# A graph layer on one core: only row tiles and one weight first, and the last layer norm from a row sum and a sum of squares

## The reference

```python
xn = layernorm(x)                                  # no gain, eps 1e-5
y  = segment_sum(edge_weight[:, None] * xn[src], dst) @ Wg + bg
q, k = elu(xn @ Wq + bq) + 1, elu(xn @ Wk + bk) + 1    # 8 heads of 64
v  = xn @ Wv + bv
mix = (q @ (k.T @ v)) / (q . sum(k)) @ Wp + bp         # per head
x  = x + y + mix
z  = layernorm(x)
g  = mean over rows(relu(z @ gfc1.T + b) @ gfc2.T + b) # 8 gates
W1m = W1 + sum_e g_e tv_W1[e];  W2m = W2 + sum_e g_e tv_W2[e]   # biases too
r  = z + relu(z @ W1m.T + b1m) @ W2m.T + b2m
out = x + (r - mean(r)) * rsqrt(var(r) + eps) * lng + lnb
```

## Time and profile before

| | us |
|---|---|
| device time, median of 3 runs | 1880.41 (1877.25 to 1880.98) |
| profiled execution, device time | 1881.32 |
| its span | 1879.5 |
| busy: TensorE, VectorE, POOL, ScalarE | 1549.2, 1212.1, 919.1, 702.8 |
| opening, head loop, k phase, q phase, last pass (from stretches) | 39, 200, 538, 579, 190 |

### The profile page before, as it was taken

How to read it: one execution, slowest core, us unless ns; L and a number is a source line. 1 busy time by engine, 2 the same in 40 slices (tenths; PEclk the granted TensorE clock), 3 DMA queues, 4 the chain that set the end, 5 groups by cost and what they waited for, 6 DMA issues and landing times.

```text
span 1879.5 us, 27602 instructions
## 1 busy us (share of the span) xinstructions
PE 1549.2 (82%) x8551; PEld 672.3 (36%) x8551; DVE 1212.1 (64%) x2230; ACT 702.8 (37%) x1098; POOL 919.1 (49%) x919
## 2 busy tenths in 40 slices
PE   0699968888988898787888888888887799888883
PEld 0345423333333333243333333333333444453331
DVE  7888734554544555456776777676667666468996
ACT  3266522222222232212332333333333677425554
POOL 3000056666666666646666666666663000016776
PEclk9799989999999999978999999999999799989996
DMA  5389777777777777746666666666665422333332
GB/s 182 127 297 324 272 238 227 220 214 224 225 227 223 227 225 225 213 123 193 194 197 200 196 195 196 195 196 197 196 197 154 159 78 79 115 115 107 134 134 83
DMA packets 149271, 353.64 MB, mean 188 GB/s; under 512 B 24773, under 2 KB 30551, under 8 KB 149155
## 3 DMA queue, kind: packets, MB, share of 16 engines
q0 software_dynamic: 62720, 205.57, 37.0%
q1 hardware_dynamic: 84926, 145.42, 22.6%
q10 hardware_dynamic: 1509, 1.21, 0.2%
HBM read 287.93 MB, written 65.38 MB: 188 GB/s over the span
## 4 chain that ended last, share of the span: by engine, by line
PE 37%; DVE 18%; another core or an unknown queue 16%; issue 14%; ACT 9%; DMA 2%; DVEq 1%; ACTq 0%; SPq 0%; POOL 0%; POOLq 0%
PE bank L1550 26%; PE bank L1659 4%; PE bank L1633 4%; ACT mb L642 2%; PE bank L1649 2%; DVE acc L1164 2%; ACT part L636 2%; DVE st L1058 1%; PE bank L1592 1%; ACT qT L663 1%; DVE res L1511 1%; DVE zr L1539 1%; DVE zl L1092 1%; ACT zh L598 1%
## 5 line engine op out<-in xcount | busy, mean ns | idle before, releaser
L850 POOL DMA_INDIRECT rows<-y_rows,idxT x784 | 767.9, 979 | 613.3 <-issue 395.1
L1164 DVE SCALAR_TENSOR_TENSOR acc<-bank,maskt,acc 128x512 f32 x392 | 275.4, 744 | 200.3 <-remote 107.4
L642 ACT ACTIVATE mb<-bank,ones,ncols 128x512 f32<-128x512 f32 x98 | 76.6, 782 | 527.5 <-remote 290.6
L1550 PE MATMUL bank<-KVP,qT 128*128 128x512 f16 x588 | 168.2, 446 | 72.1 <-ACT qT L663 62.1
L1649 PE MATMUL bank<-rows,hots 128*32 128x512 f16 x2352 | 194.3, 402 | 38.7 <-issue 35.1
L1659 PE MATMUL bank<-part,plc 128*128 128x512 f32 x392 | 212.1, 622 | 12.3 <-ACT part L636 6.0
L636 ACT COPY part<-bank 128x512 f32<-128x512 f32 x196 | 113.0, 577 | 192.7 <-remote 145.5
L1550 PE MATMUL bank<-Wg,xtb 128*128 128x512 f16 x588 | 143.3, 396 | 25.6 <-DVE xtb L1103 25.5
L1550 PE MATMUL bank<-Wk,xta 128*128 128x512 f16 x588 | 142.9, 394 | 1.2 <-issue 1.0
L1633 PE MATMUL bank<-xr,kh 128*128 128x512 f16 x392 | 124.8, 402 | 16.7 <-DVE kl L1191 13.4
L1649 PEld LDWEIGHTS bank<-rows,hots 128*32 128x32 f16 x2352 | 78.1, 143 | 166.4 <-issue 144.3
(11 more groups left out here) (278 smaller groups left out, 2324.0 us busy)
## 6 DMA issues: line engine op xcount, KB each, us to landing
xta<-xt_rows SPq DMA_DIRECT2D x98, 256.0 KB
x_rows<-xhl SPq DMA_DIRECT2D x49, 256.0 KB, 2.6
xt_rows<-xtb SPq DMA_DIRECT2D x49, 256.0 KB, 3.0
y_rows<-yb SPq DMA_DIRECT2D x49, 256.0 KB, 2.5
rows<-y_rows,idxT POOLq DMA_INDIRECT x784
xr<-x_rows SPq DMA_DIRECT2D x49, 256.0 KB
zt_rows<-ztg SPq DMA_DIRECT2D x49, 256.0 KB, 2.0
acc<-in_x SPq DMA_DIRECT2D x48, 256.0 KB, 3.1
```

Source lines behind the costliest of these rows:

```text
L642: nc.scalar.activation(mb[:, :], of[:, :], ACT.Relu, scale=ncols[:, col:col + 1], bias=ones[:, 0:1]).then_inc(f_min, 1)
L850: pool.indirect_dma_start(out=rows[:, slot].rearrange("p a d -> p (a d)"), out_offset=None, in_=y_rows, in_offset=bass.IndirectOffsetOnAxi ...
L1164: nc.vector.scalar_tensor_tensor(out=flat(acc, tile + m), in0=placed_bank(s)[:, :], scalar=maskt[:, m, s:s + 1], in1=flat(acc, tile + m), ...
L1550: ins = nc.tensor.matmul(dest, lhs, rhs, start=(n == 0 and only), stop=(n == len(pairs) - 1), skip_group_check=not only)
```

## The change

It is several changes put together.

- Opening: SyncE asks for row tiles 0 to 3, the edge lists, row tiles 4 to 7 and then biases; ScalarE's queue loads Wg alone. VectorE takes the statistics of tiles 0 to 3, the maximum of Wg and one set of scales (`y_scale`). Both parts of Wg are made in tick 0.
- Wk and Wq are loaded in the head's tick 40 (`KQ_AT`), the edge lists are packed in tick 41; maxima in ticks 42 and 43, scales (`kq_scale`) in 44, high parts in 45 and 46, low parts in 47 and 48. POOL splits both bias rows and issues their six small DMAs. The raw weights have buffers of their own.
- `x_rows` is gone. In the k phase x itself is loaded again, ScalarE normalises it again in float32 and float16 (`x_again`, ahead of keep_part in the slot), and VectorE makes the low part (`x_lower`).
- Wv is loaded after two low parts, Wp only after the last `x_lower`. graw is loaded after four turned tiles of the q phase; its maximum and scale are made 18 and 28 slots after the turn.
- W2's task vectors are loaded in pairs, (6, 7) at the tail's start, and TensorE adds pair by pair; W1's transposes stand before the last pair. VectorE's split of b2 stands after W1's parts.
- Last pass: `res` writes its row sum too, VectorE makes the negative mean, ScalarE squares res - mean with a sum, and its root makes sd. VectorE writes cen = (res - mean) * lngb and ob = cen * scale + acc. bn_stats, aggregation, nbr, ScalarE's zr and POOL's ob are gone. An output tile follows five ticks behind.

The diff, cut to its core:

```diff
 @block.sync
-for k, w in enumerate((gnn_w, Wk, Wq)):
-    sp.dma_start(stage[:, k], w.rearrange(...)).then_inc(w_loaded[k], 16)
-for r, b in enumerate((bk, bq, bp, gnn_b)):
-    sp.dma_start(brow[:, r, :], ...)
 for j in range(Q4):
     load_x(0, j)
 load_edges()
 for j in range(Q4):
     load_x(1, j)
+load_biases()
...
 def head_stores(g, j):
-    if exists(g, j):
-        t = tile_at(g, j)
-        sp.wait_ge(head.low, t + 1)
-        sp.dma_start(row_tile(x_rows, t), xhl[:, j % 4]...)
+    if isinstance(g, int) and tile_at(g, j) == KQ_AT:
+        sp.wait_ge(tabled, 3)
+        for k, (dest, w) in enumerate(((Wkraw, Wk), (Wqraw, Wq))):
+            sp.dma_start(dest[:, :, :], ...).then_inc(w_loaded[k + 1], 16)
+    if isinstance(g, int) and tile_at(g, j) == KQ_AT + 1:
+        pack_edges()
...
-sp.wait_ge(tabled, 3)
+sp.wait_ge(low_made, 2)
 sp.dma_start(Wv32[:, :, :], ...)
-sp.dma_start(Wp32[:, :, :], ...)
+sp.wait_ge(wq_low, 1)
 def load_rows(t):
     b = t % 2
-    at_least(sp, m_done, t - 1)
-    sp.dma_start(xr[:, b]..., row_tile(x_rows, t)).then_inc(xr_in[b], 16)
+    at_least(sp, xr_high, 2 * (t - 1))
+    sp.dma_start(xraw[:, b], row_tile(x[0:(T - 1) * P, :], t)).then_inc(xr_in[b], 16)
...
+sp.wait_ge(xr_low, T)
+sp.dma_start(Wp32[:, :, :], ...)
...
 @block.scalar
-for k, w16 in enumerate((Wg16, Wk16, Wq16)):
-    act.wait_ge(scales_made, 1)
-    nc.scalar.activation(w16[:, 0], stage[:, k], ACT.Copy, scale=scf[:, k:k + 1])
+act.dma_start(Wgraw[:, :, :], ...).then_inc(w_loaded[0], 16)
...
+def x_again(t):
+    b = t % 2
+    act.wait_ge(xr_in[b], 16 * (t // 2) + 16)
+    at_least(act, xr_low, t - 1)
+    at_least(act, m_done, t - 1)
+    for to in (xn32[:, b, :], xr[:, b, 0, :]):
+        nc.scalar.activation(to, xraw[:, b, :], ACT.Identity, scale=rs[:, t:t + 1], bias=nb[:, t:t + 1])
...
 def out_tick(g, j):          # ScalarE
+    nc.scalar.activation(squares[:, :], res[:, j1, :], ACT.Square, bias=negm[:, par, i:i + 1],
+                         accum_out=dev2[:, par, i:i + 1]).then_inc(squared, 1)
-    nc.scalar.activation(sd4[:, 0:n], var4[:, ..., 0:n, 1], ACT.Sqrt, bias=epsc[:, :])
+    nc.scalar.activation(sd4[:, 0:n], dev2[:, ..., 0:n], ACT.Sqrt, scale=1.0 / D, bias=epsc[:, :])
-    nc.scalar.activation(zr[:, b, :], res[:, j4, :], ACT.Identity, scale=rsr..., bias=nbr...)
...
 def out_tick(g, j):          # POOL
     pool.tensor_tensor(flat(acc, t), flat(acc, t), lnbb[:, :], ALU.add).then_inc(based, 1)
-    pool.tensor_tensor(ob[:, b, :], zr[:, b, :], flat(acc, t), ALU.add).then_inc(ob_made, 1)
...
 @block.vector
+if at == 0:        weight_low(0, Wg16, Wgraw, low_made)
+if at == KQ_AT + 2: link(weight_largest(1, Wkraw))
+if at == KQ_AT + 3: link(weight_largest(2, Wqraw)); (maximum of the bias row)
+if at == KQ_AT + 4: kq_scale()
+if at == KQ_AT + 7: weight_low(1, Wk16, Wkraw, low_made)
+if at == KQ_AT + 8: weight_low(2, Wq16, Wqraw, wq_low)
...
+def x_lower(t):
+    nc.vector.tensor_tensor(xr[:, b, 1, :], xn32[:, b, :], xr[:, b, 0, :], ALU.subtract)
...
 def out_tick(g, j):          # VectorE
     nc.vector.scalar_tensor_tensor(out=res[:, j, :], in0=bank[4 + b][:, :], scalar=cols[:, 4:5],
-                                   in1=zq[:, b, :], op0=ALU.mult, op1=ALU.add)
-    nc.vector.bn_stats(st6[:, j % Q4, :], res[:, j, :])
+                                   in1=zq[:, b, :], op0=ALU.mult, op1=ALU.add, accum_out=rsum[...])
+    nc.vector.scalar_tensor_tensor(out=cen[:, :], in0=res[:, j5, :], scalar=negm[...],
+                                   in1=lngb[:, :], op0=ALU.add, op1=ALU.mult).then_inc(gained, 1)
+    nc.vector.tensor_scalar(negm[...], rsum[...], -1.0 / D, None, ALU.mult).then_inc(mean_made, 1)
+    nc.vector.scalar_tensor_tensor(out=ob[:, b5, :], in0=cen[:, :], scalar=rsr[...],
+                                   in1=flat(acc, t5), op0=ALU.mult, op1=ALU.add).then_inc(ob_made, 1)
-    nc.vector.tensor_tensor(zr[:, b, :], zr[:, b, :], lngb[:, :], ALU.mult)
...
 @block.tensor
-pe.wait_ge(tv2_loaded, 16 * NE)
+for i, pair in enumerate(TV2_PAIRS):
+    if i == len(TV2_PAIRS) - 1:
+        (W1's transposes)
+    pe.wait_ge(tv2_loaded[i], 32)
+    for e in pair:
+        (tvW2[:, e] times its diagonal added to every block of the result)
```

More of the change, by code:

```diff
@@ L1516, in out_tick @@
[L1516 to L1517 removed]
+                                                   in1=zq[:, b, :], op0=ALU.mult, op1=ALU.add,
+                                                   accum_out=rsum[:, j // Q4, j % Q4:j % Q4 + 1]).then_inc(res_made, 1)
+                if j % Q4 == 1 and not (isinstance(quad, int) and quad == 0):
                     n, par = 1 if isinstance(quad, int) and quad == NQ else Q4, (j // Q4 + 1) % 2
```

353 lines of the change are left out of this document (201 added, 152 removed).

## The result

The changed kernel takes 1897.21 us (median of 4 runs, 1889.82 to 1905.52) against 1880.0 us before: the ratio is 1.0095, its 95% interval 1.0049 to 1.0141. Forecast were 1854 us, so the sign is wrong. The profiled execution of it took 1889.82 us (span 1887.9), the fastest of the four, and 8.5 us more than that of before; the table takes both traces apart at the same instructions, so it accounts for these 8.5 us and not for the 17.2 between the medians.

What follows compares the result with a forecast made beforehand. No single bound: TensorE bounds the head loop, VectorE the last pass, and each stage is priced alone. From the profiled 1881.3 us, -18.5 + 11 - 2.5 + 2 - 1 + 1 - 16 - 3 = -27 gives 1854, range 1832 to 1874.

Steps and rivals of the forecast that it cites:

- 1, the opening: Start of the kernel: first tick's statistics start at 20.5 us instead of 38.96, a gain of 18.5 us (14 to 22).
- 2, the end of the head loop: Head ticks 42 to 48: the work for Wk and Wq moved there adds 11 us (8 to 17).
- 3, the transition: Between head and k phase: Wp's load is gone from there, -2.5 us (-4 to +3).
- 4, the k phase: K phase: ScalarE's rebuild and VectorE's subtraction add 2 us (-3 to +10); q phase 0 (-1 to +2).
- rival C: K phase: ScalarE's rebuild lands on the chain, 0.8 us a tile, giving 1892 us; chance 0.09.
- 5, tail and combine: Tail -1 us (-2 to 0) for the gate's maximum, combine +1 us (-1 to +3).
- the b2 term: Combine: VectorE's split of b2, now after W1's low parts, ends later than W2's chain starts now; +1 us (-1 to +3).
- 6, the last pass: Last pass: a quad takes 13.5 us instead of 14.98, over eleven quads -16 us (-28 to 0).
- Rival B: Last pass stays at 15 us a quad through sharing of VectorE and POOL, giving 1870 us; chance 0.14.
- the opening's worse end: Start of the kernel: the hold of SyncE's queue stays, tick near 25 us; joined with Rival B 1878 to 1884, chance 0.04.
- 7, the drain: End of the last pass: two VectorE operations per tile replace three engines taking turns, -3 us (-6 to -1).
- Rival D: Last pass: cen and ob run at half speed, 1.25 to 1.3 us each, giving 1900 us; chance 0.02.

Runs made afterwards that it cites:

- e1: Changed kernel with POOL's addition of lnb to acc in the last pass left out (output lacks lnb): ratio 0.9958 to the kernel before.
- e3: Changed kernel with the seven edge-packing DMAs issued at the start on ScalarE's queue again: ratio 1.0105 to the kernel before.
- e5: Changed kernel with Wk and Wq loaded early on POOL's queue instead of SyncE's in tick 40: 1878.95 us, ratio 1.0062 to the kernel before.
- e4: Changed kernel with x_rows stored and loaded again, without x_again and x_lower: 1734.78 us, ratio 1.0036 to the kernel before.
- (b): Later runs on another chip, or one in another condition, with no edit implied; the kernel before takes 1727 us there.
- e6: Changed kernel with VectorE's split of b2 put back ahead of the wait for W1's transposes: ratio 1.0108 to the kernel before.
- e2: Changed kernel with POOL's additions in the last pass held until the next quad's low parts of hT are made: ratio 0.9974 to the kernel before.

## Why the prediction was wrong, point by point

**1, the opening: right.** 18.78 against 20.5, inside 16.5 to 25. The hold of SyncE's queue varies: 7.64 us in this trace. In e1's the tick starts at 25.1, in the other eleven experiments' traces with this opening between 18.7 and 20.8: the upper end was real, the lower one wasn't seen.

**2, the end of the head loop: mechanism half right, size off.** +11 forecast, +15.2 measured (205.0 - 189.8). VectorE's and ScalarE's part was right: 7.3 + 2 + 0.5 = 9.8 forecast, and from tick 40 to tick 48 the copies take 32.9 us for 23.2, 9.7 more. The term that failed is "the load of Wk and seven packing DMAs ... 1.5": the copy of tick 40 comes 10.2 us behind that of tick 39 instead of 4.8, 5.4 more. It is not the issuing queue that is held, as I priced it (e3), but the stores which VectorE's two-buffer copy waits for land late while 2 MB are loaded, and a part of that remains when these are issued elsewhere (e5).

**3, the transition: right.** -2.5 forecast, 9.1 - 12.3 = -3.2 measured. Wp's late load cost nothing that shows: it is issued at 789.9, and its first product starts at 818.8 behind others.

**4, the k phase: rival C's mechanism, at a third of its price, and in another place.** +2 was forecast; e4 gives 11, and the table 8.4 for k phase and turn. "It comes late by the gathers, not by ScalarE" was true of the copy of part and answered the wrong question. The new wait was not in the trace of before: TensorE's `m_product` now waits for the last of three operations on two engines. In the q phase "untouched but for one maximum: 0" failed: the step listed VectorE's maximum and left out POOL's reduction, which was moved into the stream of gathers. It set them back by 4.3 us at its place, and the q phase is 3.8 us longer (7.2 in (b)).

**5, tail and combine: forecast 0, measured +4.5.** The direction of the b2 term was seen, and its place (a split that ends behind the moment when W2's maxima could start). I took +1; e6 gives 4.1 for it. The tail is 1.4 us longer where -1 was forecast; no run shows why.

**6, the last pass: the step that decides.** Forecast 13.5 a quad; 15.33 measured, above even the 15.0 that the range allowed, where VectorE was to be held as much as before. The prices were about right: cen and ob 0.74 and 0.75 alone (e1), small means 0.14, ScalarE's side idle enough. VectorE's busy time came out lower than the 13.5 of the sum, at 12.52 a quad: 10.07 without the additions (e1), and 2.45 for the meetings, for which 2.6 was put down. What failed is to take that sum for the time of a quad: a sum of VectorE's busy time, in which every meeting with POOL weighs the same. VectorE is idle for 28 of 153 us. What sets the quad is a loop between two engines. From the end of the low part TensorE's product of the next quad's first tile, its hidden rows and its second tile take 6.3 us; then come VectorE's ticks 1 and 2, each with residual, cen, mean, ob and low part, 8.2 together with two slow low parts. That makes 14.5. In every second quad TensorE's part is 8.0 us, at the lower clock level for 3.4 of them, and the quad 16.4. With low parts of 0.75 and TensorE at the higher level it would be 12.5; e1 has 12.5 and 12.7 in turn. Before, the addition met the product with lngb, for which only POOL waited; now it meets, twice a quad, the one operation that TensorE waits for. "Each of which can meet one two-input operation" was written without asking which one. TensorE's floor of 12.3 was taken from a stretch at a mean granted clock of 0.93; at 1.00 its work is 11.8 a quad (e1).

Rival B named the sharing and its two rows, and gave 1870; with B, the head's 4, the k phase's 9, the reduction's 4 to 7 and the combine's 4 the sum is 1870 + 4 + 9 + 5 + 4 = 1892, between the profiled 1890 and the median 1897. (Single terms of it scatter by some us.) That B and a part of C could hold together was given no chance of its own: B was joined only with the opening's worse end, 0.04, which came to no change. Slower got 0.11, for C and D each alone, as if only one term would miss.

**7, the drain: right.** From the last whole quad's reciprocal to the end of the last output 8.4 us (1872.57 to 1881.0), before 12.3; -3.8 for -3. It is given back at the other end, where the reciprocal stands a tick later than before and the first one comes 3.6 us later.

Rival D fell: cen takes 0.74 us alone (e1), as much as the residual with one source in PSUM. The Trainium skill's "Vector Engine (DVE) Microarchitecture Reference", section 7, cited there for half the throughput, is against these rows. The Trainium skill's "VectorE: DVE Perf Modes", section "Two Vector instructions with no wait between them", cited in step 6 for two instructions, agrees with them: the residual's row sum appears as an instruction of its own, DVE_READ_ACCUMULATOR. It takes 0.08 us, not the 0.19 of ScalarE.

## What to carry to other kernels

Price a contention by which operation it hits, not by how many: before moving an operation of a shared resource, follow what releases it, see what the other engine does at that moment, and who waits for that. Where a stage has idle time on its "bounding" engine after the change, a sum of busy times is no forecast; draw the loop of waits between the engines instead. A moved step takes every engine's share with it (a reduction on POOL, loads beside the stores that a copy waits for), and each lands in somebody's list.

## What was not expected of the hardware

- Two operations that meet are both slower: VectorE's low part 1.75 us for 0.75, POOL's addition 1.49 on the mean (1.27 at its shortest).
- A 256 KB store issued behind 2 MB of loads on the same queue landed 13.2 us after its issue (e3), where the median is 2.6. With the loads on POOL's queue the store beside them still took 8.7 us (e5). What of the difference is due to the queue and what to the earlier moment wasn't tried.
- A reduction of 0.48 us on POOL between gathers was preceded by 6.08 us without another instruction than two MODIFY_POOL_CONFIG records at their start; the same pair stood 5.7 to 7.2 us ahead of it in twelve other traces.
- Short waits of TensorE went with stretches at the lower clock level: 3.4 us in every second quad of the changed kernel, none in ten quads of e1 and e2. TensorE's work of ten quads was 127.3 us in the one and 117.9 and 119.9 in the others.
- The same kernel took 1880, 1868 and 1727 us on different occasions, steady within 0.9% on each. The difference between 1880 and 1727 lies in the slots, where rows are gathered (k phase 528 against 459 us, q phase 606 against 530); the other stages agree within 1 us. Why is open, and there is no trace of the kernel before from the occasion with 1868.
